# A three-layer Perceiver kernel on one core: its prologue reordered (identity, rows of ones, first weights, scaling of x)

## What is computed

```python
x = x + _L0_xattn_ref(_layernorm(x), ctx_1024, ctx_1024, w_q, w_k, w_v, w_o)   # 16 heads of 64, 4096 keys
x = x + _L0_attn_ref(_layernorm(x), Wq, Wkv, Wo, pre_proj, post_proj, mem_k, mem_v)
x = x + _L0_ffn_ref(_layernorm(x), w_gate, w_up, w_down)                       # with quantise-dequantise steps
```

## Time and profile before

| what | value |
|---|---|
| median of three runs | 1379.91 us (1377.32 to 1381.26) |
| the profiled execution | 1378.64 us, its span 1376.9 us |
| PE busy | 1269.1 us, 92% of the span |
| DVE, ACT, Pool busy | 865.0, 880.6 and 411.5 us |
| mean granted clock of PE | 0.967 of full speed |

### The profile page before, as it was taken

The page is one execution under the profiler, slowest core; times in us unless marked ns, Lnnn a source line. Parts: engine busy times, 40 slices in busy tenths (PEclk is TensorE's granted clock), DMA queues, the critical chain, the costliest instruction groups (busy, mean ns, idle before and its releaser), DMA issues. The chain is left out here.

```text
span 1376.9 us, 21414 instructions
## 1 busy us (share of the span) xinstructions
PE 1269.1 (92%) x8447; PEld 1007.5 (73%) x8447; DVE 865.0 (63%) x1121; ACT 880.6 (64%) x1543; POOL 411.5 (30%) x373
## 2 busy tenths in 40 slices
PE   4999999999999999899999999999999969898663
PEld 4887887878787878688878787878787834667422
DVE  4547575766666576655766667676657655657366
ACT  4858586867777776566868677777768512535242
POOL 4505051524334341240514233342515012030000
PEclk9999999999999999999999999999999979998876
DMA  5000000000000001200000000000000053353000
GB/s 171 1 1 20 1 20 1 20 1 20 8 13 16 1 20 47 77 20 1 20 1 20 1 21 20 1 20 1 16 1 4 1 198 59 41 65 37 1 0 16
DMA packets 29684, 34.62 MB, mean 25 GB/s; under 512 B 3985, under 2 KB 26001, under 8 KB 29329
## 3 DMA queue, kind: packets, MB, share of 16 engines
q1 hardware_dynamic: 27536, 29.83, 8.3%
q0 software_dynamic: 2048, 3.43, 1.8%
HBM read 25.89 MB, written 0.52 MB: 19 GB/s over the span
## 5 line engine op out<-in xcount | busy, mean ns | idle before, releaser
L496 DVE TENSOR_TENSOR prob_sum<-prob_sum,probs 128x1024 f32<-128x1024 f32 x224 | 261.6, 1221 | 171.1 <-ACT probs L417 170.4
L330 POOL TENSOR_TENSOR k_split<-probs,k_split 64x512 fp32r<-64x512 f32 x128 | 164.8, 1287 | 336.8 <-ACT probs L377 335.3
L473 DVE TENSOR_REDUCE step_max<-scores_a 128x2 f32<-128x1024 f32 x128 | 156.6, 1223 | 97.2 <-PE scores_a L599 97.1
L332 POOL TENSOR_TENSOR k_split<-probs,k_split 64x512 fp32r<-64x512 f32 x128 | 164.8, 1288 | 9.6
L417 ACT ACTIVATE probs<-scores_a 128x1024 f32<-128x1024 f32 x98 | 100.5, 1026 | 93.8 <-PE scores_a L612 93.8
L473 DVE TENSOR_REDUCE step_max<-scores_b 128x2 f32<-128x1024 f32 x128 | 155.6, 1216 | 0.0
L417 ACT ACTIVATE probs<-scores_b 128x1024 f32<-128x1024 f32 x98 | 100.6, 1027 | 56.0 <-PE scores_b L612 56.0
L322 POOL TENSOR_TENSOR w_lo<-w_raw,w_hi 128x768 fp32r<-128x768 f32 x16 | 38.1, 2379 | 326.7 <-ACT w_hi L344 326.7
L623 PE MATMUL out_ps<-probs,v_far 128*64 128x256 f32 x1024 | 118.0, 382 | 0.0
L623 PE MATMUL out_ps<-probs,v_near 128*64 128x256 f32 x1024 | 118.0, 382 | 0.0
L611 PE MATMUL scores_a<-q_twice,k_split 128*128 128x256 f32 x392 | 100.3, 288 | 0.2 <-ACT probs L417 0.2
(11 more groups left out here) (218 smaller groups left out, 2871.3 us busy)
## 6 DMA issues: line engine op xcount, KB each, us to landing
ctx_rows<-in_ctx_dram SPq DMA_DIRECT2D x10, 512.0 KB, 3.8
w_raw<-in_L_xattn_w_v_dram SPq DMA_DIRECT2D x14, 256.0 KB, 3.2
probs<-in_ctx_dram SPq DMA_DIRECT2D x6, 512.0 KB, 6.2
grouped<-dots_sb SPq DMA_DIRECT2D x16, 136.0 KB
grouped<-dots_sb POOLq DMA_DIRECT2D x16, 136.0 KB, 13.2
w_raw<-in_L_xattn_w_q_dram SPq DMA_DIRECT2D x16, 128.0 KB, 2.4
w_raw<-in_L_xattn_w_k_dram SPq DMA_DIRECT2D x16, 128.0 KB, 2.4
wo_pair<-in_L_xattn_w_o_dram SPq DMA_DIRECT2D x16, 128.0 KB, 2.1
```

What stands on the lines that cost most here:

```text
L330: pool.tensor_tensor(k_split[DH:P, A, keys], staged[0:DH], k_split[0:DH, A, keys].bitcast(F32), ALU.subtract).then_inc(k_low, 1)
L332: pool.tensor_tensor(k_split[0:DH, B, keys], staged[DH:P], k_split[DH:P, B, keys].bitcast(F32), ALU.subtract).then_inc(k_low, 1)
L473: dve.tensor_reduce(step_max[:, :, 1 - h, j - 1], scores[h][:, :, :], X, ALU.max).then_inc(max_done, 1)
L496: dve.tensor_tensor(prob_sum[:, h, :], prob_sum[:, h, :], probs[:, j % 2, h, :], ALU.add).then_inc(sum_done, 1)
```

## The change

Pool no longer makes the identity. DVE does, at its very start: a memset, a ramp 0 to 31 doubled in five additions, one 32x32 block transpose, and four comparisons that set the diagonal blocks. DVE then takes the moments of x but scales x only behind context group 1, and copies the transposed x behind group 4 in place of 3. Pool fills one half of `k_ones` ahead of `invert_std`, no longer waits for DVE's scaling before it fills the other half, and writes both rows of ones itself, so ACT loses L437. ACT splits the first weights behind group 3 in place of 5. PE transposes x behind group 3 in place of 2.

```diff
--- before.py
+++ after.py
@@ -48,9 +48,7 @@
 NORMALISED = 3 * TOK_TILES
 
 
-def normalise_rows(dve, x, out, stats, moments, chain, inverse_std):
-
-
+def measure_rows(dve, x, stats, moments, chain):
     n = 0
     for t in range(TOK_TILES):
         dve.bn_stats(stats[:, t, :], x[:, t, :]).then_inc(chain, 1)
@@ -58,12 +56,20 @@
     dve.wait_ge(chain, n)
     for t in range(TOK_TILES):
         dve.bn_aggr(moments[:, t, :], stats[:, t, :]).then_inc(chain, 1)
-    n += TOK_TILES
+
+
+def scale_rows(dve, x, out, moments, chain, inverse_std):
+    n = 2 * TOK_TILES
     dve.wait_ge(inverse_std, 3)
     for t in range(TOK_TILES):
         dve.tensor_scalar(out[:, t, :], x[:, t, :], moments[:, t, 0:1], moments[:, t, 1:2],
                           ALU.subtract, ALU.mult).then_inc(chain, 1)
     assert n + TOK_TILES == NORMALISED
+
+
+def normalise_rows(dve, x, out, stats, moments, chain, inverse_std):
+    measure_rows(dve, x, stats, moments, chain)
+    scale_rows(dve, x, out, moments, chain, inverse_std)
 
 
 def invert_std(pool, moments, power, chain, inverse_std):
@@ -91,6 +97,9 @@
     PAIR = 2 * DH
     V_TILES = HALF // STEPS
     A, B = 0, 1
+    BLOCK32 = 32
+    RAMP = [1, 2, 4, 8, 16]
+    IDENT = 2 + len(RAMP) + 1 + P // BLOCK32
 
     with ExitStack() as stack:
         r = Resources(nc, stack)
@@ -132,6 +141,7 @@
         recip = prob_sum[:, A, 2 * SEQ:3 * SEQ]
         outT = r.sbuf("outT", [P, SEQ])
         ones = r.sbuf("ones", [P, DH])
+        ramp = r.sbuf("ramp", [P, 2, BLOCK32])
 
         scores = [r.psum("scores_a", [P, 2, CHUNK]), r.psum("scores_b", [P, 2, CHUNK])]
         k_both = r.psum("k_both", [P, 2, CHUNK])
@@ -145,7 +155,6 @@
         ctx_loaded = [r.sem(f"ctx_loaded{slot}") for slot in range(SLOTS)]
         w_loaded = r.sem("w_loaded")
         wo_loaded = r.sem("wo_loaded")
-        ones_a = r.sem("ones_a")
         ident_made = r.sem("ident_made")
         consts_ready = r.sem("consts_ready")
         norm_chain = r.sem("norm_chain")
@@ -302,18 +311,17 @@
 
         @block.gpsimd
         def _(pool):
-            pool.memset(ident[:, :], 0.0).then_inc(ident_made, 1)
-            pool.wait_ge(ident_made, 1)
-            pool.affine_select(out=ident[:, :], in_=ident[:, :], compare_op=ALU.not_equal, fill=1.0, base=0,
-                               pattern=[[-1, P]], channel_multiplier=1).then_inc(ident_made, 1)
             pool.memset(ones[:, :], 1.0).then_inc(consts_ready, 1)
             pool.memset(neg_max[:, :, :], 0.0).then_inc(consts_ready, 1)
-            invert_std(pool, moments, power, norm_chain, inverse_std)
-            pool.wait_ge(norm_chain, NORMALISED)
+            pool.wait_ge(consts_ready, 2)
             pool.memset(k_ones[DH:P, A, :].bitcast(F32), 0.0).then_inc(consts_ready, 1)
             pool.wait_ge(consts_ready, 3)
+            invert_std(pool, moments, power, norm_chain, inverse_std)
+            pool.wait_ge(inverse_std, 3)
             pool.memset(k_ones[0:DH, B, :].bitcast(F32), 0.0).then_inc(consts_ready, 1)
             pool.wait_ge(consts_ready, 4)
+            pool.memset(k_ones[DH:DH + 1, A, :].bitcast(F32), 1.0).then_inc(consts_ready, 1)
+            pool.wait_ge(consts_ready, 5)
             pool.memset(k_ones[0:1, B, :].bitcast(F32), 1.0).then_inc(consts_ready, 1)
 
             def body(it, b, i, parity):
@@ -332,7 +340,7 @@
                     pool.tensor_tensor(k_split[0:DH, B, keys], staged[DH:P], k_split[DH:P, B, keys].bitcast(F32),
                                        ALU.subtract).then_inc(k_low, 1)
                 pool.wait_ge(k_low, 2 * STEPS * (it + 1))
-            pool.wait_ge(consts_ready, 5)
+            pool.wait_ge(consts_ready, 6)
             for b in range(BATCH):
                 pairs_of_batch(pool, b, body)
 
@@ -431,17 +439,27 @@
                 if b == 0:
                     for n in range(LOADS):
                         context_high(act, n)
-                        if n == LOADS - 3:
+                        if n == 3:
                             split_weights(0, 0, 0)
-                    act.wait_ge(consts_ready, 5)
-                    act.activation(k_ones[DH:DH + 1, A, :], ones[DH:DH + 1, 0:1].to_broadcast([1, CTX]), ACT.Copy
-                                   ).then_inc(ones_a, 1)
                 pairs_of_batch(act, b, body)
 
         @block.vector
         def _(dve):
+            dve.memset(ident[:, :], 0.0).then_inc(ident_made, 1)
+            dve.memset(ramp[:, 0, 0:1], 0.0).then_inc(ident_made, 1)
+            for n, w in enumerate(RAMP):
+                dve.wait_ge(ident_made, 2 + n)
+                dve.tensor_scalar(ramp[:, 0, w:2 * w], ramp[:, 0, 0:w], float(w), None, ALU.add
+                                  ).then_inc(ident_made, 1)
+            dve.wait_ge(ident_made, 2 + len(RAMP))
+            dve.transpose(ramp[:, 1, :], ramp[:, 0, :]).then_inc(ident_made, 1)
+            dve.wait_ge(ident_made, 2 + len(RAMP) + 1)
+            for n in range(P // BLOCK32):
+                block32 = slice(n * BLOCK32, (n + 1) * BLOCK32)
+                dve.tensor_tensor(ident[block32, block32], ramp[block32, 0, :], ramp[block32, 1, :], ALU.is_equal
+                                  ).then_inc(ident_made, 1)
             dve.wait_ge(x_loaded, 16)
-            normalise_rows(dve, x_res, xn, stats, moments, norm_chain, inverse_std)
+            measure_rows(dve, x_res, stats, moments, norm_chain)
 
             def divide(before):
 
@@ -510,7 +528,9 @@
             for b in range(BATCH):
                 for n in range(LOADS if b == 0 else 0):
                     context_low(dve, n)
-                    if n == 3:
+                    if n == 1:
+                        scale_rows(dve, x_res, xn, moments, norm_chain, inverse_std)
+                    if n == 4:
                         for c in range(DC):
                             dve.wait_ge(xT_made, c + 1)
                             dve.tensor_copy(xnT[:, c, :], k_ps[c][:, :]).then_inc(xT_copied, 1)
@@ -521,7 +541,7 @@
         @block.tensor
         def _(pe):
             mm = pe.matmul
-            pe.wait_ge(ident_made, 2)
+            pe.wait_ge(ident_made, IDENT)
 
             def transpose_context(n):
 
@@ -674,8 +694,7 @@
                 project_v(it, b, i, parity, STEPS - 2)
 
                 if is_first(it):
-                    pe.wait_ge(consts_ready, 5)
-                    pe.wait_ge(ones_a, 1)
+                    pe.wait_ge(consts_ready, 6)
                 pe.wait_ge(max_chain, 2 * it + 2)
                 for qt in range(QT):
                     last = pe.transpose(k_ps[0][:, qt * P:(qt + 1) * P], neg_max[:, qt, :], ident[:, :])
@@ -714,7 +733,7 @@
             for b in range(BATCH):
                 for n in range(LOADS if b == 0 else 0):
                     transpose_context(n)
-                    if n == 2:
+                    if n == 3:
                         transpose_x()
                 if b == 0:
                     pe.wait_ge(xT_copied, DC)
```

## The result

The change makes the kernel slower: 1385.82 us median of six runs (1385.17 to 1388.77), beside 1380.59 of the kernel before (six runs, 1377.32 to 1382.04). The ratio is 1.0045, with a 95% interval of 1.0033 to 1.0058: some 6 us (0.0045 x 1380.6), the interval 4.6 to 8.0. The forecast was 1377.3 in a range of 1372.3 to 1380.5, no change that can be told; the measured median lies above that range. The profiled execution took 1388.77, its span 1386.9.

The account below looks back on a forecast made before the run. Bound: the prologue up to PE's restart at 36.10, since PE is full behind it. Restart 1.55 us earlier plus 1.1 from the clock, 2.65 in all, takes the median 1379.91 to 1377.3, range 1372.3 to 1380.5.

Parts of the forecast that it names:

- the choice between two engines: Prologue, DVE's four scalings of x against Pool's memset: DVE goes first, 16.9 to 18.2; the other order costs 3.5 us.
- The rival's price: Slower rival: scalings lose to Pool's memsets three times, end at 28.4, PE restarts near 42.8, time 1385.5; chance 0.05.
- The set-up: Pool's one-time wait before its first operation that is no memset, the 1/std addition: 10.5 us, from 4.9 to 15.4.
- the bound of 11.6: Upper bound in us on Pool's one-time wait, at half pace beside transfers throughout; 6.0 was the lower bound.
- The gain of 2.65 us: Whole forecast gain: 1.55 us from PE restarting earlier at the prologue's end, plus 1.1 us from the clock behind it.
- the 1.55 us of the restart: PE's restart at the prologue's end, after its idle time, comes at 34.55 in place of 36.10.
- The clock term: Clock 1.00 behind PE's restart, so first value projection 8.7 us behind it, not 9.8: 1.1 gained, bounds 0 to 1.6.
- The restart rule: PE's restart at the prologue's end follows the later of the transposes' end + 4.6 and Pool's weights + 3.7 us.
- The rule from the weights: If Pool's weights release PE at time W, PE restarts at W + 3.7; forecast W 30.85, restart 34.55.
- The identity on DVE: DVE's chain at the start: ready at 3.2, or about 6.5 if held by Pool's memset; the late one costs nothing.
- ACT's 3.62 us: ACT's row of ones, 28.96 to 32.6, goes from the path; Pool's weights then rule, the remaining saving is spare time.

Follow-up runs that it names:

- the best version: Changed kernel with Pool's wait back, a tiny addition as Pool's first operation, and weights moved ahead of some k_ones memsets: 1368.91 us, ratio 0.9921.

## Why the prediction was wrong, by its steps

**The step that failed** is the choice between two engines: "I take DVE first: its four scalings run 16.9 to 18.2 and Pool's memset is held until then." It rested on starts, 0.04 us behind the power for DVE and 0.06 to 0.08 for Pool. The starts did come in that order, 0.02 us apart, in three executions (two of the changed kernel and the kernel before without its wait), and DVE was held each time. Where the sum had the scalings run from 16.9 to 18.2, they ran from 18.46 to 31.21, and PE restarted at 45.00 in place of 34.55: of the 13.0 us by which the scalings ended late, 11.4 are the held scalings (12.75 in place of 1.38 us) and 1.6 the later 1/std. The time for which a DVE operation is held lies inside its record, behind its start, so the start does not show who won; the row at 1113.61 had that already: a record of 1.36 us for an operation of 0.41. The rival's price was right in kind: "The port is lost three times". It was given 5.6 us and a chance of 0.05, on the ground that at 1113 three scalings ran through behind one that was held. There the three memsets had no wait between them, were over behind the first scaling, and nothing of Pool's followed; here Pool waits on a semaphore between its memsets, and one scaling passes at each gap. No run takes those waits out, so that they let the scaling pass is argued from the two traces and not shown. The prediction named that mechanism and then weighed it by a row that could not show it. A fourth turn, against the split of the weights, was in no case at all; the scalings ended at 31.2 in place of the rival's 28.4, of which 1.6 us are the later start. That the rival's 1385.5 lies so near the measured 1385.82 is in part luck: its restart of 42.8 was 2.2 us early.

**The set-up** was placed right and sized wrong. It stands before whichever operation comes first that is no memset, it starts when Pool arrives, and only once: shown by moving it, and by the second layer's affine_select, which has none. The 10.5 us was 12.1, above even the bound of 11.6. That bound took the third layer's 6.01 as the undisturbed length and one pace wherever transfers run. The undisturbed length was 7.0 to 7.6, but with it the same working gives only 11.1 to 11.3: it is the single pace that does not hold, and what else makes the late set-up long stays open. The trace agrees with the Trainium skill (GPSIMD Engine Reference, Instruction dispatch) that there is such a cost at a first call, without an instruction of its own; that it is a load of code no run here shows. Its 6 us is that of the third layer here, 1 to 1.6 under this one's undisturbed length and half of what it costs beside a full set of transfers. On the port the trace agrees with the Trainium skill (SBUF - State Buffer, Who interferes with whom) that the one that loses stands still for the whole of the other's instruction. The same section gives the pair to whoever issues first; the records here show starts and not issues, and DVE, which started 0.02 us ahead each time, lost, so the rule could not be used to say who wins.

**The gain of 2.65 us** was too large as well: with the wait put back, and so with the race decided as the forecast had it, the time is that of before (0.4 us under, the interval 1.9 under to 0.8 over). Of the 1.55 us of the restart 0.17 came, since the set-up was 0.95 longer than forecast and the low clock ahead of the restart took 0.45 more. The clock term held: from the restart to the first value projection it is 8.4 to 8.9 us in the seven executions in which the pair of matmuls at the restart took under 1 us, 8.7 forecast, against 9.6 to 10.3 in the five in which it took 1.22 us, before among them.

**The restart rule** held to 0.2 us wherever the clock was high: transposes end + 4.6 gives 45.1 in the changed kernel (measured 45.00) and 25.7 in the best version (25.56). The rule from the weights misses by 0.5 to 1.3 us where PE idles 2.5 us or more ahead of them, because part or all of the two projections behind runs at the low clock: the term that the rule left out.

**Two more steps held.** The identity on DVE costs nothing and gives nothing by itself, and ACT's 3.62 us did not come back where Pool's weights became later by as much.

## What to carry to other kernels

Where VectorE and GpSimd both touch SBUF, a semaphore wait that seems to cost GpSimd time may be what keeps it out of VectorE's way: before dropping one, look for a copy or tensor_scalar between two SBUF tiles on VectorE in the same stretch, and where GpSimd waits between its operations, price one of them for each VectorE operation, not one for all. GpSimd's first operation that is no memset owed a set-up of 7 to 12 us in every version here; put a tiny one at the very start of the program, and order the rest of GpSimd's work by who waits for it, filling by memset last. Here the wait put back and these two orders turned the change's loss of some 6 us into a gain of 10.7.

## What the runs showed of the hardware

A VectorE tensor_scalar of 128x256 float32, SBUF to SBUF, does not run beside a GpSimd memset or a GpSimd tensor_tensor between SBUF tiles. It was held each of the eleven times in the prologue that one of these was under way or just starting (three memsets and the split of the weights in each of two executions of the changed kernel, three memsets in the kernel before without its wait): 3.67 us behind a memset in place of 0.41, the first of each series though its record was the first to start. Memsets of a single partition (1x4096) hold it as long as those of 64, 3.54 and 3.50 us.

VectorE operations that read from PSUM were not held: two of DVE's low parts, with one input in PSUM, take 1.28 us beside the memset of the earlier trace rows and 1.29 in the changed kernel at 9.21, where Pool stands in its set-up.

Tiny operations are held as well: five additions on 1 to 16 columns took 4.29 us beside a memset of 3.51, and 0.98 without it.

GpSimd's set-up was 7.0 and 7.6 us with few or no transfers beside it, 8.2 to 8.7 when it started at 0.9 us, 10.2 to 11.2 when it started at 1.0 to 1.2, and 11.5 to 12.1 when it started at 4.9 and the transfers lasted through nearly all of it (DMA share 1.0 up to 14 us and 0.8 from 14 to 17).
